# Layer norms of an audio tower: centering by one matmul with the identity minus the average

## The reference

```python
def _layernorm(x, axis=-1, eps=1e-05):
    m = jnp.mean(x, axis=axis, keepdims=True)
    v = jnp.var(x, axis=axis, keepdims=True)
    return (x - m) / jnp.sqrt(v + eps)

h = _L0_tok_ref(x)
h = h + _L0_attn_ref(_layernorm(h, axis=-1), ...)
h = h + _L0_ffn_ref(_layernorm(h, axis=-1), ...)
...
h = h + _L3_ffn_ref(_layernorm(h, axis=-1), ...)
```

## Time and profile before

| | |
|---|---|
| median of three runs | 2384.0 us |
| the profiled execution | 2378.89 us |
| its span in the trace | 2376.9 us |
| granted TensorE clock, mean over the span | 0.872 of full speed |
| PE busy | 1839.4 us (77%) |
| DVE busy | 1656.8 us (70%) |
| ACT busy | 1326.2 us (56%) |
| POOL busy | 1045.0 us (44%) |

### The profile page before, as it was taken

How to read it: one execution, slowest core, us unless ns; L and a number is a source line. 1 busy time by engine, 2 the same in 40 slices (tenths; PEclk the granted TensorE clock), 3 DMA queues, 4 the chain that set the end, 5 groups by cost and what they waited for, 6 DMA issues and landing times. The chain is left out here.

```text
span 2376.9 us, 49583 instructions
## 1 busy us (share of the span) xinstructions
PE 1839.4 (77%) x19188; PEld 1360.2 (57%) x19188; DVE 1656.8 (70%) x2544; ACT 1326.2 (56%) x2658; POOL 1045.0 (44%) x811
## 2 busy tenths in 40 slices
PE   4788898888878765557647887777577599999997
PEld 3344444444433333335446777556566489999997
DVE  1599999999999983438295442326434478888886
ACT  2767777777767543013334444232355378888885
POOL 0377777777678750530005777200250023333332
PEclk8899999999999996558668999688687599999998
DMA  2344444444444421510025888300650231121000
GB/s 72 123 135 127 130 143 136 124 135 128 132 135 134 132 75 30 104 27 1 15 90 163 265 256 250 108 1 2 219 156 5 66 135 59 59 71 70 17 4 21
DMA packets 91293, 240.81 MB, mean 101 GB/s; under 512 B 16362, under 2 KB 39476, under 8 KB 88500
## 3 DMA queue, kind: packets, MB, share of 16 engines
q1 hardware_dynamic: 76612, 212.20, 28.7%
q0 software_dynamic: 9408, 18.93, 3.6%
q10 hardware_dynamic: 5040, 6.52, 0.8%
HBM read 222.30 MB, written 15.30 MB: 100 GB/s over the span
## 5 line engine op out<-in xcount | busy, mean ns | idle before, releaser
L874 POOL TENSOR_TENSOR dBu<-du,Bs 128x858 f32<-128x858 f32 (+1 forms) x240 | 588.2, 2453 | 228.5 <-DVE hst L798 101.5
L395 PE MATMUL py<-hst,ident 128*128 128x429 f32 (+1 forms) x960 | 415.6, 563 | 97.8 <-DVE hst L808 97.2
L798 DVE TENSOR_TENSOR_SCAN hst<-dA,dBu 128x858 f32<-128x858 f32 (+1 forms) x240 | 458.6, 1911 | 22.8 <-ACT dA L690 22.0
L1866 POOL DMA_INDIRECT xi<-token_rows,take x152 | 148.3, 976 | 542.5 <-POOLq L90 497.1
L690 ACT ACTIVATE dA<-dt,negA 128x416 f32<-128x416 f32 (+1 forms) x480 | 269.6, 596 | 185.5 <-DVE hst L798 184.1
L395 PEld LDWEIGHTS py<-hst,ident 128*128 128x128 f32 x960 | 183.6, 202 | 295.8 <-DVE hst L808 170.8
L2388 POOL TENSOR_TENSOR hm<-h,mw 128x264 f32<-128x264 f32 x128 | 90.4, 706 | 432.0 <-DVE h L2369 432.0
L808 DVE TENSOR_TENSOR hst<-hst,Cs 128x858 f32<-128x858 f32 (+1 forms) x240 | 247.5, 1031 | 0.0
L2284 PE MATMUL pg<-hs,wh 128*128 128x68 f16 x6144 | 215.2, 195 | 19.4 <-DVE hs L2372 16.3
L1961 ACT ACTIVATE eh<-ph,wb 128x128 f32<-128x128 f32 x480 | 136.8, 367 | 152.3 <-PE ph L1896 152.3
L2284 PE MATMUL pg<-xm,wi 128*128 128x68 f16 x6144 | 214.2, 195 | 4.5 <-issue 3.2
(11 more groups left out here) (395 smaller groups left out, 3364.8 us busy)
## 6 DMA issues: line engine op xcount, KB each, us to landing
wb<-sf_w SPq DMA_DIRECT2D x96, 514.0 KB, 4.8
Bs<-bc_rows SPq DMA_DIRECT2D x96, 429.0 KB, 4.7
Cs<-bc_rows SPq DMA_DIRECT2D x96, 429.0 KB, 3.5
mw<-route_weights SPq DMA_DIRECT2D x8, 2112.0 KB
wb<-gf_w SPq DMA_DIRECT2D x24, 514.0 KB, 5.0
Bs<-bc_rows SPq DMA_DIRECT2D x24, 396.0 KB, 5.0
Cs<-bc_rows SPq DMA_DIRECT2D x24, 396.0 KB, 4.3
mb<-route_masks SPq DMA_DIRECT2D x8, 1088.0 KB, 5.6
```

Source lines behind the costliest of these rows:

```text
L395: return nc.tensor.matmul(out, weight, moving, **kw)
L798: v.tensor_tensor_scan(hst[:, g % HR, 0:2 * n], dA[:, g % 2, 0:2 * n], dBu[:, g % 2, 0:2 * n], 0.0, ALU.mult, ALU.add).then_inc(h_ready, 1)
L874: g_.tensor_tensor(dBu[:, g % 2, 0:2 * n].rearrange("p (a n) -> p a n", a=2), du[:, j % 2, :, 0:n], Bs[:, q % NBS, k % BG, 0:n].unsqueeze( ...
L1866: pool.indirect_dma_start(xi[:, j % UN, :], None, xs, bass.IndirectOffsetOnAxis(ap=take[:, j:j + 1], axis=0)).then_inc(taken[j % UN][0], 16)
```

## The change

The mean matmul and VectorE's subtraction become one matmul. The new constant `cst["cen"]` is the identity minus the average, so a matmul with it leaves x - mean in PSUM. It stays there, in three units of two banks (`cen_ps`), until it is scaled: ScalarE's square and VectorE's scale both read PSUM, and VectorE writes the destination only once. To make room `var_ps` is down to one unit of two banks. The orders become

- TensorE: center 0, center 1, var 0, center 2, var 1, center 3, var 2, var 3
- VectorE: scale 0, 1, 2, 3
- ScalarE: as before

The waits change with the buffers: center 3 waits until scale 0 has read unit 0, var c waits until the Ln of chunk c-1 has read the only variance unit. The semaphore `mean_ready` is gone, and one 64 KB constant is loaded more at the start.

```diff
-        mean_ps = psum(nc, ctx, "mean_ps", [128, 2, 2, BANK], F32)
-        var_ps = psum(nc, ctx, "var_ps", [128, 2, 2, BANK], F32)
+        cen_ps = psum(nc, ctx, "cen_ps", [128, 3, 2, BANK], F32)
+        var_ps = psum(nc, ctx, "var_ps", [128, 2, BANK], F32)
...
-            def mean(c):
-                if c >= 2:
-                    pe.wait_ge(centered, c - 1)
+            def center(c):
+                if c >= 3:
+                    pe.wait_ge(scaled, c - 2)
                 for h in range(2):
-                    last = nc.tensor.matmul(mean_ps[:, c % 2, h, 0:HB], cst["avg"], halves(part(src, c))[:, h, :],
-                                            start=True, stop=True)
-                last.then_inc(mean_ready, 1)
+                    last = nc.tensor.matmul(cen_ps[:, c % 3, h, 0:HB], cst["cen"], halves(part(src, c))[:, h, :], start=True, stop=True)
+                last.then_inc(centered, 1)
 
             def var(c):
                 pe.wait_ge(squared, c + 1)
-                if c >= 2:
-                    pe.wait_ge(logged, c - 1)
+                if c >= 1:
+                    pe.wait_ge(logged, c)
...
-            mean(0)
+            center(0)
+            center(1)
             for c in range(NCH):
-                if c + 1 < NCH:
-                    mean(c + 1)
                 var(c)
-
-        @block.vector
-        def _(dve):
-            def center(c):
-                dve.wait_ge(mean_ready, c + 1)
-                nc.vector.tensor_tensor(halves(part(dst, c)), halves(part(src, c)), mean_ps[:, c % 2, :, 0:HB],
-                                        ALU.subtract).then_inc(centered, 1)
...
-            center(0)
-            for c in range(NCH):
-                if c + 1 < NCH:
-                    center(c + 1)
-                scale(c)
+                if c + 2 < NCH:
+                    center(c + 2)
...
-                nc.scalar.activation(sq[:, c % 2, :], part(dst, c), ACT.Square).then_inc(squared, 1)
+                nc.scalar.activation(halves(sq[:, c % 2, :]), cen_ps[:, c % 3, :, 0:HB], ACT.Square).then_inc(squared, 1)
...
+        @block.vector
+        def _(dve):
+            for c in range(NCH):
+                dve.wait_ge(rstd_ready, c + 1)
+                d, x, r = halves(part(dst, c)), cen_ps[:, c % 3, :, 0:HB], halves(rstd[:, c % 2, :])
+                if gain is None:
+                    nc.vector.tensor_tensor(d, x, r, ALU.mult).then_inc(scaled, 1)
+                else:
+                    nc.vector.scalar_tensor_tensor(out=d, in0=x, scalar=gain, in1=r, op0=ALU.mult, op1=ALU.mult).then_inc(scaled, 1)
+                    dve.wait_ge(scaled, c + 1)
+                    nc.vector.tensor_scalar(part(dst, c), part(dst, c), shift, None, ALU.add).then_inc(shifted, 1)
...
+    c["cen"] = np.eye(128, dtype=np.float32) - c["avg"]
...
-            for name in ("ident", "avg", "eps"):
+            for name in ("ident", "avg", "cen", "eps"):
```

## The result

The changed kernel took 2350.4 us (median of 4 runs, 2348.31 to 2357.2) against 2383.86 (4 runs, 2380.57 to 2385.44): ratio 0.9866, 95% interval 0.9843 to 0.989. Its profiled execution took 2348.94 us with a span of 2347.1, 29.8 less than the span before. The predicted 2353.6 us and the forecast -30.4 stand beside -33.5 between the medians and -29.95 between the two profiled executions.

The account below looks back on a forecast made before the run. The norms were taken as bound by a loop through ScalarE and VectorE, not one full engine. Terms -(6.0 + 11.6 + 3.3 + 8.2) - 0.7 + 0.45 - 1 = -30.4 us took 2384.0 to 2353.6 us, range 2346 to 2364.

Parts of the forecast that it names:

- The limit: In the ten norms: no engine is full; one loop through ScalarE and VectorE takes 3.30 us per chunk.
- The start of a norm: Up to Ln 0: variance 0 still stands behind center 1, Ln 0 comes 0.23 us earlier, or nothing at half clock.
- the norms with gain: Two norms whose shift lengthens today's loop by 0.59 us: Ln 0 to last scale 11.50 to 7.52, saving 8.2 us.
- The loop: Ln to Ln in a norm: 1.91 us, once longer as center 3 waits for scale 0; saves 1.83 us per norm.
- the 2.1 that I had named as a sign of being wrong: Ln to Ln in the changed profile: a loop over 2.1 us would show the prediction wrong.
- The last variance: End of a norm: the clock holds, so four plain norms save 0.9 us more each, 11.6 us in all.
- The four plain norms: Norms at 908, 1600, 1651 and 1793 us with a slow last variance: 2.9 us saved each, 11.6 together.
- Reading PSUM: Scale and square reading PSUM: 0.71 us and 0.69 us; ends 0.05 us less to 0.15 us more per operation.
- The rival with ScalarE as the bound: PSUM reads make ScalarE the bound in the norms: loop 2.07 us, kernel 2361 us; chance 0.12.
- Barriers and constant: Barrier behind each norm, one semaphore fewer: -0.7 us in all; one more constant load at the start: +0.45 us.
- The clock behind the norms: Six stages behind norms that start with matmuls may find the clock still up: -1 us, bounds 0 to -3.
- The rival of a PE at half clock: PE at half clock throughout the norms becomes the bound; slower, 2388 us; chance 0.03.

Follow-up runs that it names:

- centers ahead: Kernel before with VectorE's centers two chunks ahead, all 40 subtractions kept: 2408.47 against 2448.3 us; repeated, 2410.41 against 2446.8 us.
- the spare matmuls: Kernel before plus four spare matmuls of 264 columns per norm between variance 2 and variance 3: 2436.02 against 2448.3 us, ratio 0.995.

## Why the prediction was right

**The limit.** "It is one loop through ScalarE and VectorE": shown. Taking center out of the loop without taking its work away gave all of the gain and more (centers ahead), so what bounded a norm was the order of VectorE's list; the new matmul is one way of breaking the loop, not the cause.

**The start of a norm.** Variance 0 behind center 1, Ln 0 4.52 us after the start instead of 5.03 in the norm at 1130 us. I had 0.23 us from this, it was 0.5 here: the first eight rows took 3.56 us instead of 3.67, and the variance straight behind them 1.05 instead of 1.16. At 1144 us it was the other way round: variance 0 ran at half clock (1.97 us), and Ln 0 came at 5.69 after 5.22 before. That is about half of the 0.9 us missing in the norms with gain; the rest is mostly in their laps, 6.33 us where I had 6.13.

**The loop.** Laps of 1.91, 2.31, 1.91 were forecast and 2.01, 2.25, 2.01 measured: 6.27 us from Ln 0 to Ln 3 against 6.13. The variance starts 0.85 us after the Ln ahead of it, not 0.72: I had taken the time from Ln to Exp, both on ScalarE, for the time from Ln to a matmul on TensorE. The first lap at 1144 us, 2.13 us behind a center 2 that began at half clock, is just over the 2.1 that I had named as a sign of being wrong; it is the only such lap besides the second ones, which were forecast at 2.31. Both waits were in the places named: the single variance unit and center 3 behind scale 0.

**The last variance.** The clock held to the end in all ten norms, and the spare matmuls showed in the kernel before what that alone is worth: 6 to 7 us of norms. The four plain norms gave 12.7 instead of 11.6, the excess being the norm that began at full clock.

**Reading PSUM.** Here a term was mis-sized, at no cost. The two lines that read PSUM, and the one with gain:

```profile
L162 ACT ACTIVATE sq<-cen_ps 128x528 f32<-128x528 f32 x40 | 24.2, 605 | 16.1 <-PE cen_ps L138 16.1
...
L183 DVE TENSOR_TENSOR xn<-cen_ps,rstd 128x528 f32<-128x528 f32 x32 | 22.6, 708 | 99.3 <-ACT rstd L175 99.3
...
L185 DVE SCALAR_TENSOR_TENSOR h<-cen_ps,c,rstd 128x528 f32<-128x528 f32 x8 | 6.1, 768 | 22.5 <-ACT rstd L175 22.5
```

VectorE's scale takes 708 ns from PSUM and 709 from SBUF; the estimated 65 ns more by the Trainium skill (VectorE: DVE Perf Modes, the section on the TRN2 errata) are not there. ScalarE's square takes 605 ns from PSUM against 0.64 us from SBUF, 0.04 less, where I took 0.05 more from comparing Ln with Exp. These differ in more than where they read: the function is another, and Ln alone adds a bias per partition. The same table's 52 cycles less for ScalarE, an estimated 43 ns, agree with the trace. The rival with ScalarE as the bound falls with this: its square costs less, not more, and ScalarE still idles 0.28 us for the variance ahead of an Ln (1134.42, 1138.68).

**Barriers and constant.** -0.72 for -0.7, and +0.31 for +0.45.

**The clock behind the norms.** The one term that failed in its reason. I took -1 us for stages that would start while the clock is up. Taken together they don't, without help: TensorE still idles for some 3 us after the last variance, and the stages together changed by -0.2 us, two of them by +1.5 and +2.1. Keeping TensorE busy through that time shows how much lay there: 7 to 10 us of the kernel, not the 0 to 3 that I gave as bounds, though a part of it came back in norms.

**How near the number is.** The closeness of the sum is in part luck. The terms that missed, +0.9 for the norms with gain and +0.8 for the clock behind the norms against -1.1 for the plain norms, nearly cancel. And I took the profiled execution to lie 5.1 us below the median after the change too; it lay 1.5 below, which is why the medians differ by 33.5 and the profiled executions by 29.95.

The rival of a PE at half clock was not met. Its price was a little low: half of 3.52 us for the first two groups is in no row, rows 3 give 3.57 from the first row to variance 0, and the norm at 908 us, at half clock throughout its start, 3.65. Slower was to be had, though by another mechanism than the one named: two centered units instead of three, +26 us.

## What to carry to other kernels

Follow the loop in a timeline before pricing the work in it: an operation that sits in an in-order list behind one it does not depend on can cost more than its duration; here moving it ahead cost nothing and gained 36 to 40 us. An operand kept in PSUM until its last use holds its unit through the whole chain; with one unit too few that chain becomes the lap. Where a stage ends with one engine's tail and the next starts with matmuls, a few spare matmuls that end before the tail does are worth a try, provided that they don't outlast it.

## What the hardware showed that I had not expected

- Four spare matmuls (1.94 us of rows) behind each norm were worth 7 to 10 us of the kernel, with either way of centering; behind the last norm the first 64 matmul rows of the next stage took 6.16 us, with centering by the matmul 4.09, after eight of them 5.09, and 6.99 to 7.39 in the nine traces without any spare matmul.
- A square of 128x528 from PSUM took ScalarE 605 ns against 643 from SBUF.
- A semaphore more in a stage costs 0.071 us at its end, whether anyone waits for it or not.
- The same kernel took some 64 us more on the chips of the later runs (2448 against 2384). In the profiled executions, which differ by 74 us, 47 of them are in the one stage ahead of the norm at 1540 us and some 1 in the norms. Why is not shown.
